# Two-layer graph kernel on one core: score parts split as columns in PSUM, one bf16 product for the rows, banks and queue orders set anew

## The reference

```
h = relu(layernorm(x))
# graph attention, 4 heads: per head Wh = h W;  e[i,j] = leaky(Wh[i].a1 + Wh[j].a2), masked by adj; softmax over j
h2 = elu(concat_heads(attn @ Wh))                   # [.., 1024]
# one more attention layer, one head, 1024 -> 256 features
out = elu(attn2 @ (h2 W_out))
y = relu(out w1 + b1) w2 + b2 + out
x = x + layernorm(y) * gamma + beta
# second block
h = relu(layernorm(x));  mi = h Wi^T;  mj = h Wj^T
x = x + deg * (mi + b) + adj @ mj
```

## Time and profile before

| | before |
|---|---|
| median of three executions | 907.75 us |
| the profiled execution | 909.05 us |
| its span, first to last instruction | 907.2 us |
| PE busy | 836.8 us, 92% |
| PEld busy | 776.6 us, 86% |
| DVE busy | 757.1 us, 83% |
| POOL busy | 703.9 us, 78% |
| ACT busy | 683.0 us, 75% |
| chain that ended last, by engine | PE 66%, DVE 17%, issue 9% |

### The profile page before, as it was taken

The page is one execution under the profiler, slowest core; times in us unless marked ns, Lnnn a source line. Parts: engine busy times, 40 slices in busy tenths (PEclk is TensorE's granted clock), DMA queues, the critical chain, the costliest instruction groups (busy, mean ns, idle before and its releaser), DMA issues.

```text
span 907.2 us, 20067 instructions
## 1 busy us (share of the span) xinstructions
PE 836.8 (92%) x6281; PEld 776.6 (86%) x6281; DVE 757.1 (83%) x1998; ACT 683.0 (75%) x1801; POOL 703.9 (78%) x948
## 2 busy tenths in 40 slices
PE   2699999999999999999999999999999999999964
PEld 1589989889998988999898899889889998989952
DVE  4978888898888889888888988888899888897753
ACT  3788878787777878778787877778777877877541
POOL 3587988877788887778888777888877788888852
PEclk9999999999999999999999999999999999999987
DMA  8100010111111011111101111110111111000000
GB/s 246 59 1 24 25 36 2 36 36 36 35 37 35 1 36 36 36 36 36 34 4 36 36 36 36 36 35 3 35 37 36 36 37 35 2 24 25 25 24 23
DMA packets 30136, 31.50 MB, mean 35 GB/s; under 512 B 1856, under 2 KB 28992, under 8 KB 30032
## 3 DMA queue, kind: packets, MB, share of 16 engines
q1 hardware_dynamic: 29776, 29.63, 10.5%
q0 software_dynamic: 256, 0.59, 0.3%
HBM read 21.82 MB, written 8.39 MB: 33 GB/s over the span
## 4 chain that ended last, share of the span: by engine, by line
PE 66%; DVE 17%; issue 9%; POOL 3%; ACT 2%; DMA 1%; SPq 0%; DVEq 0%; POOLq 0%; ACTq 0%
PE ps L1201 59%; DVE g_parts L598 4%; PE ps L1319 3%; DVE wo L711 2%; DVE lend L737 2%; PE ps L1275 2%; PE ps L1393 2%; DVE mj_lo L768 1%; DMA lend<-in_L_gnn_a_heads 1%; ACT mj_hi L1086 1%; DVE c_st L568 1%; DVE g_rest L589 1%; DVE g_parts L621 1%; DVE f_rep L669 1%; PE ps L1341 1%
## 5 line engine op out<-in xcount | busy, mean ns | idle before, releaser
L363 POOL TENSOR_TENSOR h_lo<-h2v,h_hi 128x512 fp32r<-128x512 f32 x128 | 166.6, 1302 | 0.1
L1201 PE MATMUL ps<-gh_hi,wh_hi 128*128 128x256 f32 x512 | 153.7, 300 | 1.6 <-DVE h2v L641 1.1
L1201 PE MATMUL ps<-wo_hi,h_hi 128*128 128x258 f32 x512 | 150.6, 294 | 0.0
L1201 PE MATMUL ps<-wo_lo,h_hi 128*128 128x258 f32 x512 | 145.1, 283 | 0.0
L1201 PE MATMUL ps<-wo_hi,h_lo 128*128 128x258 f32 x512 | 145.0, 283 | 0.0
L1201 PE MATMUL ps<-gh_lo,wh_hi 128*128 128x256 f32 x512 | 142.9, 279 | 0.0
L1201 PE MATMUL ps<-gh_hi,wh_lo 128*128 128x256 f32 x512 | 142.7, 279 | 0.0
L369 POOL TENSOR_SCALAR h2e<-h2e 128x512 f32<-128x512 f32 x128 | 86.2, 681 | 32.0 <-ACT h2e L959 31.8
L1201 PEld LDWEIGHTS ps<-wo_lo,h_hi 128*128 128x128 f32 x512 | 97.4, 190 | 4.3
L1201 PEld LDWEIGHTS ps<-wo_hi,h_hi 128*128 128x128 f32 x512 | 96.8, 189 | 4.6 <-POOL h_lo L363 0.4
L970 ACT ACTIVATE lend<-lend,zm 128x128 f32<-128x128 f32 x256 | 99.1, 393 | 0.0
(11 more groups left out here) (166 smaller groups left out, 2794.3 us busy)
## 6 DMA issues: line engine op xcount, KB each, us to landing
xa<-in_x SPq DMA_DIRECT2D x32, 256.0 KB, 3.1
xr<-in_x SPq DMA_DIRECT2D x32, 256.0 KB, 3.0
out<-res SPq DMA_DIRECT2D x32, 256.0 KB, 2.2
lend<-in_L_gnn_W_heads SPq DMA_DIRECT2D x4, 256.0 KB, 5.7
lend<-in_L_gnn_a_heads SPq DMA_DIRECT2D x4, 256.0 KB, 8.4
wo<-in_L_gnn_W_out SPq DMA_DIRECT2D x1, 1024.0 KB, 11.2
l1w_sb<-in_L_gnn_W SPq DMA_DIRECT2D x1, 512.0 KB, 9.7
lend<-in_L_gnn_w SPq DMA_DIRECT2D x2, 256.0 KB, 3.0
```

What stands on the lines that cost most here:

```text
L363: pool.tensor_tensor(h2_lo[:, u, :, :].rearrange("p c n -> p (c n)"), h2v[u % 2][:, :], h2_hi[:, u, :, :].rearrange("p c n -> p (c n)").bi ...
L1201: return pe.matmul(out_, lhs, rhs, start=start, stop=stop)
```

## The change

Both layers now split the scores while they are columns. DVE copies the fp32 columns out of PSUM (for the later addition), rounds them to bf16 into `parts[0]`, subtracts that from the columns **in place in PSUM**, rounds to `parts[1]`, subtracts again to `parts[2]`: five instructions on 128 partitions by 16 elements (4 in the second layer). The parts lie in a 128x128 bf16 tile whose other columns stay zero, and one bf16 product with the bf16 identity makes the rows. One copy (ACT for the first layer, DVE for the second) rounds nothing and moves them to `f_parts` and `g_parts`, from where `scores` and `scores2` read as before.

```
-            def less_first(name, p, psum, parts, rest):
...
-            def third(name, p, parts, rest):
...
+            def split_cols(name, p, cols, whole, parts):
+
+                dve.tensor_copy(whole, cols).then_inc(S[name[0]], 1)
+                dve.tensor_copy(parts[0], cols).then_inc(S[name[1] + "_first"], 1)
+                wait(dve, name[0], p)
+                wait(dve, name[1] + "_first", p)
+                dve.tensor_tensor(cols, cols, parts[0], ALU.subtract).then_inc(S[name[1] + "_rest"], 1)
+                wait(dve, name[1] + "_rest", p)
+                dve.tensor_copy(parts[1], cols).then_inc(S[name[1] + "_second"], 1)
+                wait(dve, name[1] + "_second", p)
+                dve.tensor_tensor(parts[2], cols, parts[1], ALU.subtract).then_inc(S[name[1] + "_third"], 1)
+
+            def f_cols_split(p):
 
                 wait(dve, "cols_done", p)
                 wait(dve, "rows_done", p, lag=1)
...
+                split_cols(("cols_copied", "rows"), p, ps[:, B_COLS, 0:COLS], f_cols[p.e][:, :],
+                           [f_split[p.e][:, k * COLS:(k + 1) * COLS] for k in range(3)])
+
+            def wh2_scores(p):
+
+                wait(dve, "wh2_copied", p)
+                wait(dve, "rows2_done", p, lag=1)
+                split_cols(("wh2_scores_copied", "rows2"), p, ps[:, B_WH2[0]:B_WH2[0] + 2, F:WO], g_cols[p.e][:, :, :],
+                           [g_split[p.e][:, k * COLS:k * COLS + 4].rearrange("p (b j) -> p b j", b=2) for k in range(3)])
+
+            def rows2_copy(p):
                 wait(dve, "rows2_done", p)
-
                 wait(dve, "scores2_done", p, lag=2)
-                dve.tensor_copy(g_parts[p.e][:, :], ps[:, B_ROWS2, 0:P]).then_inc(S["rows2_first"], 1)
+                dve.tensor_copy(g_parts[p.e][:, :], ps[:, B_ROWS2, 0:P]).then_inc(S["rows2_copied"], 1)
...
-            def f_first(p):
+            def rows_copy(p):
                 wait(act, "rows_done", p)
                 wait(act, "scores_done", p, lag=1)
-                act.activation(f_parts[p.e][:, :], ps[:, B_ROWS, 0:P], ACT.Copy).then_inc(S["rows_first"], 1)
+                act.activation(f_parts[p.e][:, :], ps[:, B_ROWS, 0:P], ACT.Copy).then_inc(S["rows_copied"], 1)
...
-                wait(pe, "cols_copied", p)
-                wait_bank(p, ("cols_copied", 1, 0))
-                pe.transpose(ps[:, B_ROWS, 0:P], f_rep[p.e][:, :], ident[:, :]).then_inc(S["rows_done"], 1)
+                wait(pe, "rows_third", p)
+                wait_bank(p, ("scores2_masked", 1, 3), ("hidden_full", 2, 4), ("mj_lo", 1, 6), ("scores_masked", 1, 1))
+                mm(ps[:, B_ROWS, 0:P], f_split[p.e][:, :], ident_bf[:, :], True, True).then_inc(S["rows_done"], 1)
...
-                pe.transpose(ps[:, B_ROWS2, 0:P], f2_rep[p.e][:, :], ident[:, :]).then_inc(S["rows2_done"], 1)
+                wait(pe, "rows2_third", p)
+                wait_bank(p, ("ht_copied", 1, -3), ("scores_masked", 2, -2), ("at_lo", 1, -1), ("rows2_copied", 1, 1))
+                mm(ps[:, B_ROWS2, 0:P], g_split[p.e][:, :], ident_bf[:, :], True, True).then_inc(S["rows2_done"], 1)
```

More of the change, by code:

```diff
@@ L154, in build @@
         ht = same("ht", [P, C, 2 * P])
-        f_rep = two("f_rep", [P, P])
+        f_cols = two("f_cols", [P, COLS])
+        f_split = same("f_split", [P, P], BF16)
         f_parts = same("f_parts", [P, P], BF16)
-        f_rest = same("f_rest", [P, P])
         zm, zs, zr = (two(n, [P, 2, H]) for n in ("zm", "zs", "zr"))
@@ L440, in one @@
             def one(pairs):
[L441 to L474, removed]
                 if p := pairs[3]:
                     elu_less(p, 2)
+                    h2_low(p, 1)
                     elu_less(p, 3)
-                    h2_low(p, 1)
+                if p := pairs[0]:
+                    rstd1(p)
                 if p := pairs[5]:
@@ L788, in one @@
             def one(pairs):
+                if (p := pairs[1]) and p.is_first():
+                    selectors()
+                if p := pairs[4]:
+                    gh_low(p, 3)
+                if (p := pairs[3]) and p.is_first():
+                    out_dots(1)
+                if (p := pairs[0]) and p.is_first():
+                    adj_cast()
+                if p := pairs[3]:
+                    soft_sum(p, 0)
+                if p := pairs[5]:
+                    wh2_scores(p)
+                if (p := pairs[3]) and p.is_first():
+                    out_dots(2)
@@ L1110, in one @@
                     gh_high(p, 1)
[L1111 to L1112 removed]
+                if p := pairs[6]:
+                    mj_high(p, 1)
                 if p := pairs[4]:
@@ new lines, in one @@
+                if p := pairs[1]:
+                    score_cols(p)
+                if p := pairs[3]:
+                    h2_unit(p, 0, 0)
+                if p := pairs[4]:
+                    score_rows2(p)
+                if p := pairs[3]:
+                    h2_unit(p, 0, 1)
+                if p := pairs[5]:
+                    ffn_out(p)
+                if p := pairs[3]:
+                    h2_unit(p, 1, 0)
+                if p := pairs[6]:
+                    h3_transposes(p)
@@ new lines, in one @@
+                if p := pairs[4]:
+                    scores2(p)
+                if p := pairs[3]:
+                    h2_unit(p, 1, 1)
+                if p := pairs[2]:
+                    prob_transposes(p, 0)
+                if p := pairs[1]:
+                    score_rows(p)
+                if p := pairs[5]:
+                    ffn(p, 0)
+                    ffn(p, 1)
+                if p := pairs[2]:
+                    prob_transposes(p, 1)
+                if p := pairs[3]:
+                    h2_unit(p, 2, 0)
+                    h2_unit(p, 2, 1)
```

507 lines of the change are left out of this document (224 added, 283 removed).

## The result

The changed kernel takes 883.2 us (median of 4 runs, 878.96 to 885.15), the kernel before 908.16 us on the same chip; the ratio is 0.972, 95% interval 0.968 to 0.976. Run again beside the second set of experiments (5 runs) it took 883.5 us, ratio 0.973, interval 0.971 to 0.975. The forecast was 882.0, range 874 to 898. The profiled execution took 885.15 us with a span of 883.4, against 907.2 before.

What follows compares the result with a forecast made beforehand. PE's own stream sets the pace, with a wait before scores2 for the held L598. Span 907.2 - 28.6 + 2.8 = 881.4 us, plus 1.85 around it 883.3, so 882 for the median; range 874 to 898.

Steps and rivals of the forecast that it cites:

- The wait and its cause: PE's scores2 waits for DVE's L598, held by POOL's L390 that hidden_whole releases; 1.02 us lost each time.
- The layout of the period: PE's new order timed from the last wh2, with the DVE, ACT and POOL chains; scores2 at 5.4 us.
- The spare time of the copy: Second layer's rows2_copy on DVE ends at 4.6 us, 0.8 us before scores2 needs it.
- Rival (A): Wait before scores2 only shortened: ACT 1.2 us later than laid out leaves 0.4 a period; 894 us, chance 0.15.
- The price of the split: Five small DVE instructions at 0.20 us each, start to start, so 1.0 us for a split.
- Rival (D): New DVE instructions held by POOL like L598: near 1030 us; milder form, one held, near 907, chance 0.03.
- Two products for two transposes, 0: On PE, bf16 products replacing fp32 transposes cost the same: 0, bounds 0.11 us gained or 0.1 lost.
- rival (B): Transposes on PE count with their whole 0.27 us row, so removing two gains 17 us more: 865, chance 0.03.
- Rival (C): POOL's queue becomes the bound at soft 1, holding up ffn and h2 2: slower, 926 us, chance 0.09.
- Ten short groups instead of nine, +2.8 us: PE's period gains one group of short products, each followed by 0.09 us extra: 31 x 0.09 = 2.8 us more.
- The number of waits won, 28: Waits of scores2 for L598 that disappear: 28 of 1.02 us each, 28.6 us; the last lies in the drain.
- The head, 0 between -4 and +6: Setup work dealt out anew before the first h2: taken as 0, realistically 4 us won or 6 lost.

Runs made afterwards that it cites:

- x1: Kernel before with only g_third moved ahead of hidden_whole in DVE's step: 885.3 us, ratio 0.974.
- x2: Kernel before, its old banks and queue orders kept, with the new column split and bf16 product: 891.3 us, ratio 0.981.
- x7: x2 with score_rows2 moved behind the first half of h2 unit 0 on PE: 890.7 us, ratio 0.981.
- x10: Changed kernel with ten small unused DVE reductions, about 2 us, ahead of rows2_copy: 922.0 us, ratio 1.0142.
- x8: Changed kernel with three small unused DVE reductions, 0.6 us in all, ahead of rows2_copy: 883.3 us, ratio 0.972.
- x4: Changed kernel with the split's remainder kept in an SBUF tile in place of PSUM: 894.1 us, ratio 0.985.
- x3: Changed kernel with fp32 split tiles and two fp32 transposes for the bf16 products, low two parts left out: 882.0 us, ratio 0.972.
- x6: Changed kernel with nine unused 512-column products in PE's head, five before the third pair's score_cols, four before the first h2: 880.0 us, ratio 0.970.
- x5: Changed kernel unaltered, run again as the yardstick: 883.5 us.
- x9: x7 with the third normalization's aggregate (norm3_var) ahead of the second layer's split on DVE: 887.0 us, ratio 0.974.

## Why the prediction was right, and where it was off

*The wait and its cause: right.* By the earlier trace rows it was 1.02 us in each steady period, made by L598 held behind L711. x1 moves that one line and the wait goes, with L598 at 289 ns. One reading was loose: the two instructions don't end together, L598 ends at 505.58 and L390 at 505.42.

*The layout of the period: right, to within 0.2 us for most.* From the end of the last `wh2`: `score_rows2` 3.0, measured 3.02; end of `rows2_copy` 4.6, measured 4.41; `scores2` 5.4, measured 5.41; end of POOL's `soft` 1 4.7, measured 4.57; end of `hidden_low` 6.0, measured 5.8; `elu` 0 done 7.7, measured 7.5; `h2` 2 8.7, measured 8.6. The one wrong hop is the second layer's split: forecast from 0.9 to 1.9, it ran from 1.5 to 2.4, because it stands behind `gh_low` 3 on DVE, which I had not laid out. Its spare time ahead of `score_rows2` is 0.6 us and not 1.1. x2 and x7 show what that place can cost in an order that doesn't cover it.

*The spare time of the copy: right.* 0.8 us forecast, 0.9 by x10, and x8's 0.6 cost nothing. Rival (A), the wait shortened but not gone, needed 1.2.

*The price of the split: right.* 1.0 us forecast, 0.86 measured, 132 to 183 ns for one instruction. By the page of the Trainium skill that the prediction quotes ("VectorE: DVE Perf Modes", on the TRN2 errata) one was an estimated 0.14 us: near, and a little low. Rival (D), the new instructions held, does not occur; x4 shows that it would have for one of the five in most pairs, the second rounding or the first subtraction, had the remainder been kept in SBUF. The reason given against (D) was too wide: it read L589 as the form with one SBUF input, but that line also has an input in PSUM. L594 of the first layer, a rounding with one input, from SBUF, was held in the kernel before, 921 ns (median). What the runs show free of it has an input in PSUM. Its milder form, near 907, is not what that costs: x4's two held instructions lengthen the second layer's split by 0.84 us (821 + 349 against 162 + 171), 0.6 of which was spare, and the time is 894.

*Two products for two transposes, 0: right.* x3 bounds it at 0.02 us a period, so rival (B), 17 us or 12, falls: the 0.27 of the row is a length, and what counts is the 0.11 from start to start.

*Rival (C), POOL's queue:* `soft` 1 ended on time, and no wait of PE for `elu` or `hidden_low` recurs in the steady part.

*Ten short groups instead of nine, +2.8 us: the count was right, the sum wrong.* The long products behind a short group that are 0.08 to 0.09 late are nine in a period of before (737.7 to 764.2) and ten in one of after (742.2 to 767.6). But a period of before lost 0.08 us elsewhere, at the first of `out2`'s eight short products (0.19 us to the next, where it is 0.11 in the changed kernel), and its 26 products of 512 columns were 0.04 us dearer together. The forecast put these at nothing. Without the term the period is 26.45 - 1.02 = 25.43, and 25.39 was measured.

*The number of waits won, 28: too many.* 25 steady periods gained 1.06 each, less 0.9 in a few that were longer: 25.6 us. In the three periods before them, while the pipeline fills, the changed kernel gained nothing. The longer ones have a cause in the trace that the forecast didn't look at, the input. In eight steady pairs DVE waits for the load of `x`, 4.8 us in all; in the steady part of before it never does. The three longest of these waits, 0.66, 0.96 and 1.47 us, lie in the three distances that are longer by 0.2, 0.3 and 0.8 us. The longest, in the timelines of DVE and PE:

```profile
644.31 0.75 DVE L565 BATCH_NORM_STATS2 a_st<-xa 128x6 f32<-128x256 f32 x2 [1.47 <-DMA xa<-in_x]
...
646.02 0.22 PE L1165 MATMUL ps<-ident_bf,f_split 128*128 128x128 bf16 x1 [0.71 <-DVE l1w_sb L653]
```

The statistics of `x` stand ahead of `score_mask2` (L653) on DVE, and `score_rows` on PE waits for that one by its bank. x1, with one line moved, has eight such waits of DVE too (5.0 us), x2 has 25 (15.4 us), x4 one of 0.2 us and x10, with its longer period, none. So they don't belong to the new orders alone; what makes a load late isn't shown.

*The head, 0 between -4 and +6: the size was off.* It and the filling periods cost 1.15 + 1.46 = 2.6 us more than before. x6, in which the clock stays at 1.00, reaches the fourth `score_cols` at 59.19, earlier than the 60.45 of before: so the lower clock in the head, behind two waits of PE that have grown to 1.3 us each, is what turned a small gain into a loss. The first `h2` came at 42.72 against 43.27. The 1.46 is one long distance, 28.06 us against 26.6 in x3 and x6: the granted clock is 0.88 and 0.84 there in the stretches from 102 to 114 us, and 1.00 in x3 and x6. The two places, 61.60 to 59.19 and 28.06 to 26.55, make 3.9 us; the medians of x6 and x5 differ by 3.5, but the traces have other differences behind the head, as said above.

*The drain:* 0 forecast, -0.8 measured. That says little: the same kernel took 115.8 us for it in the first profile, at a mean granted clock of 0.90, and 113.4 in x5's, at 0.93.

In the spans: 881.4 forecast, 2.8 too much for the groups, 3.0 too much gained for the waits (28.6 against 25.6), 2.6 too little for the head, 0.8 too little gained in the drain; 881.4 - 2.8 + 3.0 + 2.6 - 0.8 = 883.4. The forecast of the time came within 1.2 us because terms that are each off by nearly 3 us partly cancel, and to that extent it was luck.

What the parts of the change are worth, then: the wait is gone in every order tried here in which L598 or its successor doesn't run beside that POOL instruction. Of the new split, the place of the remainder in PSUM decides (11 us); the kind of the product does not. The new orders win 5.2 us over x1 in the 25 steady periods (636.2 us against 641.4), and the head, up to the seventh pair's `score_cols`, takes 4.1 us of it back (131.4 us against 127.3). The times are 883.2 and 883.5 us against 885.3, and the intervals of the ratios overlap: that the whole rewrite is faster than the one line moved is not shown.

## What to carry to other kernels

A short instruction that is held by another engine is first moved, before it is rewritten: look which instruction releases the one that holds it, and put the held one ahead of that. When a wait is taken away and the period doesn't move, lay the starts of successive products side by side: two waits abreast hide each other, and a wait shorter than a product's modelled length is in no list. After any change of orders the head deserves a look of its own, the granted clock above all: two waits of a good microsecond there, and the lower clock behind them, put the fourth pair 2.4 us later than in x6. And where the engines have become earlier, look again at what waits for a load.

## What the runs showed of the hardware that was not expected

- A DVE cast of 128x4 from SBUF is held to the end of a POOL instruction that began ahead of it: 969 to 972 ns in 26 of 32 pairs of x4, against 162 on average from PSUM. I had expected only the two-input subtractions to be held. They are, 826 to 1009 ns in the five pairs in which they began early in a POOL instruction, and four elements a partition are enough for it.
- The granted clock fell to the lower level at 44 to 48 us in the changed kernel, and for a time between 42 and 50 us in the five runs made from it without the filling (x3, x4, x5, x8, x10). It didn't in before, x1, x2, x7 and x9, which have the old order in the head, nor in x6. A second fall, from 106.5 us on, came in the changed kernel and not in x3, although from 102 to 106.5 us PE is busy 3.58 of 4.50 us in the one and 3.59 in the other, with one wait of 0.92 and 0.91 us. What decides between these two stays open.
- The runs of one kernel spread by up to 0.7% (878.96 to 885.15 for the changed kernel; two clusters in x9), against 0.4% for the kernel before (906.0 to 910.0 in nine runs beside x5 to x8). Two parts of it can be read from traces. The same kernel's spans of 883.4 us and 880.7 us (x5) differ by 2.4 us behind the last `score_cols`, where the mean granted clock is 0.90 and 0.93. And late loads of `x` lengthen single periods: four of them, by 3.6 us together, in x6. Why the clock and the loads differ from one execution to the next isn't known.
